# A fused attention and mixture-of-experts kernel: the list of expert tiles made in two parts, the shared expert inside the attention steps

## The reference, cut to what matters

```
x = x + attention(layernorm(x), ctx) + ctx          # per batch: theta, phi, softmax, g, norm over the batch, relu, out
n = layernorm(x)                                    # 2048 tokens of 256
scores = softmax(n @ Wg.T)                          # 16 experts in 4 groups
topi   = top 4 experts within the best 2 groups
y = sum over topi of scores * (silu(n @ W1.T) * (n @ W3.T)) @ W2.T      # 176 hidden columns per expert
z = (silu(n @ Ws1.T) * (n @ Ws3.T)) @ Ws2.T                             # the shared expert, 352 hidden columns
out = x + y + z
```

## Time and profile before

| what | value |
|---|---|
| median of 3 runs | 393.83 us |
| the profiled execution | 395.37 us, of which the profiled span is 393.2 us |
| busy in the span | PE 315.7 us (80%), DVE 254.3, ACT 189.5, POOL 188.1 |
| attention steps and shared expert units | 0 to 223 us |
| first matmul of an expert tile | 222.98 us |
| tiles at an even pace of 1.61 us | 257 to 355 us |
| loading back the ranks, sums, output | 354.8 to 393.2 us |

### The profile page before, as it was taken

The page is one execution under the profiler, slowest core; times in us unless marked ns, Lnnn a source line. Parts: engine busy times, 40 slices in busy tenths (PEclk is TensorE's granted clock), DMA queues, the critical chain, the costliest instruction groups (busy, mean ns, idle before and its releaser), DMA issues.

```text
span 393.2 us, 9572 instructions
## 1 busy us (share of the span) xinstructions
PE 315.7 (80%) x2620; PEld 242.3 (62%) x2621; DVE 254.3 (65%) x923; ACT 189.5 (48%) x473; POOL 188.1 (48%) x223
## 2 busy tenths in 40 slices
PE   0699899967999399954559885499999999999573
PEld 0377577746777287643448653377777777777352
DVE  3456877768775977776877461266665666665584
ACT  0555756652656335742210251366766666665410
POOL 1543332100565235663155665756665666665450
PEclk9999999986989778965589999699999999999969
DMA  8902312220243332352128687688768866678996
GB/s 282 370 14 72 121 65 66 66 64 14 97 130 116 108 92 84 101 203 71 56 92 302 169 181 145 155 146 165 157 143 138 172 149 149 157 172 259 342 323 219
DMA packets 82540, 58.28 MB, mean 148 GB/s; under 512 B 58954, under 2 KB 75981, under 8 KB 82512
## 3 DMA queue, kind: packets, MB, share of 16 engines
q1 hardware_dynamic: 62928, 38.81, 36.6%
q0 software_dynamic: 6912, 17.84, 15.1%
q10 hardware_dynamic: 12672, 1.27, 2.6%
HBM read 24.97 MB, written 24.53 MB: 126 GB/s over the span
## 4 chain that ended last, share of the span: by engine, by line
PE 23%; DVE 8%; SPq 8%; issue 7%; DMA 6%; POOL 5%; ACT 0%; DVEq 0%; ACTq 0%; POOLq 0%
PE banks L815 9%; PE bank L833 8%; POOL slot_rows L1577 5%; SPq L481 4%; PE bank L815 3%; DMA slot_rows<-rows_all,slot_k 3%; SPq L470 3%; DMA w<-ranked 2%; DVE x_all L1515 1%; DMA ranked<-ctx_all 1%; DVE w L1091 1%; SPq L475 0%; PE banks L821 0%; PE bank L821 0%; PE banks L823 0%
## 5 line engine op out<-in xcount | busy, mean ns | idle before, releaser
L1641 POOL DMA_INDIRECT ranked<-ctx_all x80 | 84.0, 1050 | 53.3 <-issue 36.5
L1577 POOL DMA_INDIRECT slot_rows<-rows_all,slot_k x64 | 63.9, 998 | 31.7 <-issue 16.6
L815 PE MATMUL banks<-w,ctx_all 128*128 x324 | 57.3, 313 | 3.8 <-DMA ctx_all<-slot_rows 3.8
L833 PE MATMUL bank<-w,hT 128*128 (+1 forms) x400 | 57.8, 277 | 2.2 <-ACT ctx_all L624 2.2
L755 PE MATMUL banks<-xT_all,w 128*118 128x128 f16 (+1 forms) x576 | 45.8, 252 | 0.0
L755 PEld LDWEIGHTS banks<-xT_all,w 128*118 128x118 f16 x576 | 44.6, 165 | 0.4
L624 ACT ACTIVATE ctx_all<-bank,ctx_all 128x256 f32<-128x256 f32 x80 | 37.7, 472 | 9.8 <-DMA ranked<-ctx_all 4.9
L815 PEld LDWEIGHTS banks<-w,ctx_all 128*128 128x128 f16 x324 | 31.2, 98 | 18.1 <-DMA ctx_all<-slot_rows 5.2
L833 PEld LDWEIGHTS bank<-w,hT 128*128 128x128 f16 (+1 forms) x400 | 36.3, 99 | 5.5 <-issue 2.5
L1382 DVE TENSOR_TENSOR hh<-hid,hh 128x48 f16<-128x48 f32 x80 | 16.7, 208 | 34.5 <-ACT hh L592 34.1
L592 ACT ACTIVATE hh<-hid 128x176 f16<-128x176 f32 x80 | 27.9, 349 | 16.5 <-DVE hid L1378 15.5
(11 more groups left out here) (174 smaller groups left out, 673.7 us busy)
## 6 DMA issues: line engine op xcount, KB each, us to landing
wst<-w_dram SPq DMA_DIRECT2D x18, 608.0 KB, 4.0
w<-ranked SPq DMA_DIRECT2D x16, 512.0 KB, 9.6
x_all<-x_dram SPq DMA_DIRECT2D x4, 512.0 KB, 7.8
ctx_all<-ctx_dram SPq DMA_DIRECT2D x1, 1536.0 KB, 10.7
out_dram<-x_all SPq DMA_DIRECT2D x3, 512.0 KB, 4.1
slot_rows<-pad_rows SPq DMA_DIRECT2D x9, 144.0 KB
ctx_all<-slot_rows ACTq DMA_DIRECT2D x80, 1.0 KB
ranked<-ctx_all POOLq DMA_INDIRECT x80
```

The source lines that it names most:

```text
L815: i = mm(U[j][:, 0:UP1], xt(2 * part + k), up_at(wcol, k, wpart), start=k == 0 and (wpart, part) == (0, 0), stop=k == 1 and wpart == 1)
L833: i = mm(y[:, 0:T], hT[0:rows, j, k * P:(k + 1) * P], down_at(wcol, rows, col), start=start and n == 0, stop=stop and n == len(DOWN) - 1)
L1577: G.indirect_dma_start(scatter_rows, bass.IndirectOffsetOnAxis(ap=slot_k[:, b * TOPK + k:b * TOPK + k + 1], axis=0), rows32[:, b * ROW32:( ...
L1641: G.indirect_dma_start(ranked, bass.IndirectOffsetOnAxis(ap=pair(m)[1], axis=0), y_sb[:, m % YR, :], None, bounds_check=(TOPK + 1) * TOKEN ...
```

## The change

The list of tiles is made twice. The first table has 32 tiles (`FIRST_TILES`), all of them full, from the tokens of the first twelve batches; it is made in the attention steps 18 to 20. The second has the other 48 and is made in expert turns 6 to 12, after the group of batches 12 to 15, whose slots are now computed in turns 3 and 4. Counted on the reference's routing, the first twelve batches fill 40 tiles, and the thresholds of `done_i` (the tiles after which a rank is complete: 60, 64, 68, 72) are the same in both kernels. All 16 shared units are in the steps; unit 15 goes down and is added in turns 0 and 2. Batches 8 to 11 are routed as the loop routes its groups. The pads move from in front of the tiles to SP in front of tiles 16 and 24. POOL sends 48 of its 64 scatters before the tiles, 6 before the first placed tile and 10 between placed tiles 1 to 19. The expert loop of PE has 24 turns in its body instead of 32.

```diff
-FUSED = 10
+FIRST_TILES = 32
-        EARLY = B - 2 * Q
+        EARLY = B - Q
@@ SP
-            issue_pads(sp, 0, NE // 2)
-            sp.wait_ge(S["table_ready"], 1)
-            sp.wait_ge(S["scattered"], 16 * EARLY * TOPK)
-            sp.wait_ge(S["tails_in"], 16 * (NE + 1))
+            sp.wait_ge(S["scattered"], 16 * EARLY * TOPK)
+            sp.wait_ge(S["table_ready"], 1)
...
-            for t in range(2 * MR):
+            for t in range(FIRST_TILES):
+                if t in (2 * MR, 3 * MR):
+                    issue_pads(sp, (t - 2 * MR), (t - MR))
                 if t % 4 == 0:
                     first = load_four(sp, row_i[:, t:t + 4], SLOTS)
-                    sp.wait_ge(places_landed, sp.value_load(places_i[:, t + 3:t + 4], min_val=1, max_val=TOPK))
                 load_tile(t, t % MR, first[t % 4])
-            sp.wait_ge(places_landed, TOPK)
+            sp.wait_ge(S["table_ready"], 2)
+            sp.wait_ge(last_scattered, 16 * (B - EARLY) * TOPK)
+            sp.wait_ge(S["tails_in"], 16 * (NE + 1))
@@ ACT, step
                 tile(s, v, 2, exps)
+                group(s, v, 9, route_exp)
                 tile(s, v, 5, copy_xT)
-                tile(s, v, UP_LAG, shared_tanh, count=FUSED)
+                tile(s, v, UP_LAG, shared_tanh)
                 tile(s, v, 1, theta_phi)
                 tile(s, v, 2, copy_pT)
-                if isinstance(s, int) and s >= B:
-                    tile(s, v, 10, lambda b, u: u == 0 and route_exp(b))
-                else:
-                    group(s, v, 9, route_exp)
@@ DVE, step
                 group(s, v, 10, slots_by_rank)
-                routing(s, v, route_sum)
+                group(s, v, 9, route_recip)
+                group(s, v, 9, route_score)
+                group(s, v, 9, group_max)
+                if isinstance(s, int) and s == B + 3:
+                    full_tiles()
                 tile(s, v, 3, latent_out)
-                routing(s, v, route_recip)
...
@@ DVE, expert turns
+                if r is None and s == 2:
+                    shared_add(B - 1, (B - 1) % 4)
+                if r is None and s == 3:
+                    slots(b0)
+                    count_tokens()
                 estep(s, v, r)
+                if r is None and s == 3:
+                    slots_by_rank(b0)
+                if r is None and s == 4:
+                    slots_sum(b0)
+                    slots_out(b0)
+                if r is None and s == 6:
+                    tiles_up_to(P - 1)
+                if r is None and s == 7:
+                    other_tiles()
+                if r is None and s == 8:
+                    other_rows()
@@ DVE, the first table
+            def full_tiles():
+                V.memset(ones_e[:, :], 1.0)
+                tiles_up_to(0)
+                V.tensor_scalar(taken[:, :], ntc[:, :], float(FIRST_TILES), None, ALU.min)
+                V.tensor_scalar(still[:, :], ntc[:, :], float(FIRST_TILES), -1.0, ALU.min, ALU.mult)
...
+                tile_rows(first_t, 0)
@@ POOL
-                tile(s, v, 11, scatter_two(0), count=EARLY)
+                tile(s, v, 11, scatter_two(0), count=EARLY - 3)
...
+            for b in range(EARLY - 3, EARLY):
+                for k in range(TOPK):
+                    send(b, k, S["scattered"])
+            sends = iter([(b, k) for b in range(EARLY, B) for k in range(TOPK)])
             routed(EARLY)
-            send_place(0, EARLY, B - Q)
...
+            for _ in range(6):
+                send(*next(sends), last_scattered)
...
-            for t in range(MR):
-                place_tile(t, t)
+            for t in range(LONG):
+                place_tile(t, t % MR)
+                if t % 2 == 1 and t < 20:
+                    send(*next(sends), last_scattered)
```

More of the change, by code:

```diff
@@ L743, in router, with shared_up @@
                 i.then_inc(S["l_mm"], 1)
-            def shared_up(b, u, chunks=range(SC)):
-                of = units_at(b) if isinstance(b, int) else UX
+            def shared_up(b, u):
+                if isinstance(b, int) and b == B - 1:
+                    pe.wait_ge(SH["h_ready"], b)
                 if isinstance(b, int) and b == 0:
                     pe.wait_ge(S["wl_ready"], 2)
-                for chunk in chunks:
+                for chunk in range(SC):
                     for half in range(2):
@@ L784, in step @@
                 tile(s, v, 3, mean_all)
-                drain = isinstance(s, int) and s >= B + 2
-                if not drain:
-                    group(s, v, 10, count)
-                if isinstance(s, int) and s == B + 2:
-                    pe.wait_ge(S["thph_ready"], B)
-                    pe.wait_ge(S["p_ready"], B)
-                    shared_up(FUSED, FUSED % 4, (0,))
+                group(s, v, 10, count)
                 tile(s, v, 1, theta)
                 tile(s, v, 5, transpose_rows)
-                tile(s, v, UP_LAG, shared_up, count=FUSED)
+                tile(s, v, UP_LAG, shared_up)
                 tile(s, v, 1, phi)
@@ L895, in estep @@
                     weights.load(s - 4, step_v - 4)
+                if r is not None and step_v == FIRST_TILES - LONG:
+                    pe.wait_ge(S["table_ready"], 2)
                 if has(s, 0) and step_v % 4 == 0:
@@ L1020, in latent_all @@
                 dve.wait_ge(S["st_mm"], b + 1)
-                if u == 3 and not isinstance(b, int):
+                if u == 3 and (not isinstance(b, int) or b == B - 1):
                     dve.wait_ge(S["pre_mm"], b - 3)
@@ L1252, in shared_add @@
                 xs = x_all[:, span(b * T, T)]
-                V.tensor_tensor(xs, sum_at(b) if isinstance(b, int) else YG, xs, ALU.add).then_inc(SH["y_ready"], 1)
+                V.tensor_tensor(xs, YG, xs, ALU.add).then_inc(SH["y_ready"], 1)
             def step(s, v):
-                if isinstance(s, int) and s >= B + 2:
-                    return drain(s)
+                ending = isinstance(s, int) and s >= B + 2
                 late(s, v, 5, low)
@@ L1262, in step @@
                 tile(s, v, 3, latent_stats)
-                tile(s, v, ADD_LAG, shared_add, count=FUSED)
+                tile(s, v, ADD_LAG, shared_add)
                 group(s, v, 10, chosen_diff)
@@ L1287, in step @@
                 tile(s, v, 3, latent_out)
-                routing(s, v, route_recip)
-                tile(s, v, 3, weights_low, count=NU)
-                routing(s, v, route_score)
+                group(s, v, 9, group_compare)
+                if not ending:
+                    tile(s, v, 3, weights_low, count=NU)
                 group(s, v, 10, token_weights)
-                routing(s, v, group_max)
+                group(s, v, 9, group_equal)
                 group(s, v, 10, destinations)
-                routing(s, v, group_compare)
+                group(s, v, 9, group_before)
@@ L1295, in step @@
                 group(s, v, 10, slots_sum)
                 tile(s, v, 4, normalise2)
-                routing(s, v, group_equal)
+                group(s, v, 9, group_rank)
                 group(s, v, 10, slots_out)
                 late(s, v, 2, add_context)
-                routing(s, v, group_before)
-                tile(s, v, UP_LAG, shared_gate, count=FUSED)
-                routing(s, v, group_rank)
+                group(s, v, 9, group_choose)
+                if isinstance(s, int) and s == B + 4:
+                    tile_table(1, 0, FIRST_TILES)
@@ L1303, in step @@
+                tile(s, v, UP_LAG, shared_gate)
+                group(s, v, 9, mask_mult)
                 tile(s, v, 2, recip)
-                routing(s, v, group_choose)
-                tile(s, v, UP_LAG, shared_product, count=FUSED)
-                routing(s, v, mask_mult)
+                group(s, v, 9, mask_add)
+                tile(s, v, UP_LAG, shared_product)
+                group(s, v, 9, top_values)
                 tile(s, v, 3, relu_low)
-                routing(s, v, mask_add)
@@ L1376, in hidden @@
+                group(s, v, 9, top_four)
+                group(s, v, 9, top_replace)
+                if ending:
+                    tile(s, v, 3, weights_low, count=NU)
             def hidden(G, n, j, m):
@@ L1604, in step @@
                     tile(s, v, 2, add_context)
-                tile(s, v, 11, scatter_two(2), count=EARLY)
+                tile(s, v, 11, scatter_two(2), count=EARLY - 3)
             for s in range(B + 4):
```

308 lines of the change are left out of this document (93 added, 215 removed).

## The result

The change takes 383.46 us in the median of 4 runs (380.71 to 389.41), the kernel before 395.21 us (392.82 to 397.25): ratio 0.968, 95% interval [0.958, 0.978]. Measured twice more beside other kernels it gave 0.977 [0.967, 0.987] and 0.964 [0.959, 0.969]. The forecast of 379.7 against 393.83 is 0.964. The trace shown here is that of the third measurement, of the same kernel, 382.45 us with a span of 380.6 us.

The account below looks back on a forecast made before the run. It took DVE's wait for ACT's routing exponential to bound loop routing steps and POOL to bound from 188 us. Terms -9.8, +1.3, +3.7 and -9.3 sum to -14.1 us: 393.8 becomes 379.7 us, range 374 to 390.

Parts of the forecast that it names:

- loop steps, exponential in front: Steps 9 and 13: routing exponential ahead of ACT's copy removes DVE's wait; 4.9 us a group with clock, -9.8 us together.
- last steps: Softmax 15 to the last statistics: a routing group and shared units inserted there make 19.24 us into 22.9, +3.7 us.
- T0 to `slot_k`: From tile 0's first up to the last group's `slot_k`: 7.1 us to the fourth product plus 2.0, 9.1 us.
- behind tile 20: Everything after POOL places tile 20, 115 us of turns and final sums: same instructions in both kernels, no change.
- the stall changes its name: Rival, steps 9 and 13: DVE waits for POOL's `rstd` or PE's rows instead, steps stay 15 us; 389.5 us, chance 0.08.
- The clock that comes back: PE's clock behind the loop's routing steps: recovery worth between nothing and 3.5 us a group, taken as 1.2.
- last steps at half clock: Rival, last steps: PE stays near half clock, shared units cost 5.8 us more in four steps; 385.5 us, chance 0.14.
- POOL's order behind the last `rstd`: From last `rstd` to tile 20: 14 sends before the tiles instead of 32, 10 between them; -9.3 us.
- The landing: Time from the start of the last send before the tiles until it has landed: 3.8 us taken.
- Sends beside DVE: Rival, last `rstd` to tile 20: 50 sends and placings take 0.25 us longer each, 12.5 us; 392.2 us, chance 0.03.
- Units don't overlap (slower): Rival, last steps: each unit lengthens its step by 3.5 us, so last `slot_k` decides; 399.4 us, chance 0.06.
- The covers: Hidden work: DVE's routing before tile 0's product (3 us spare), SP's pads (cost 0), turn 32 behind the sends (1 us spare).

Follow-up runs that it names:

- the exponential alone: Kernel before, with ACT's routing exponential put in front of the copy of transposed rows in loop steps 9 and 13 only; ratios 0.983 and 0.975.
- putting it back: The change with the routing exponential again behind ACT's copy in loop steps 9 and 13; 394.18 us, 0.994.
- the sends first: The change with all 16 sends of the last group ahead of the first placed tile, instead of 6; 390.84 us, 0.986.
- the transpose before down: The change with PE's `transpose_h` in step 18 in front of the router and the shared unit's down; 383.08 us, 0.971.
- all three edits: The change with last group's slots ahead of tile 0, step 18's transpose before down, two sends before the last `rstd`; 0.957, then 382.05 us, 0.942.
- The single edits: The change with one edit each: last group's slots ahead of tile 0 (0.966), step 18's transpose before down (0.971), three sends before the last `rstd` (0.962).
- the three sends earlier: The change with three of the 14 sends behind POOL's last `rstd` put in front of it; 380.68 us, 0.962.
- the three edits with late pads: All three edits, with SP's second eight pads moved from in front of tile 24 to behind tile 31; 384.11 us, 0.957.

## Why the prediction was right

The measured median lies in the range, and the order of the steps held. How well each term fits depends on the execution, so both traces of the change are shown that can be compared, the third measurement's and the second's:

| step | predicted | third | second |
|---|---|---|---|
| loop steps, exponential in front | -9.8 | -9.8 (-8.76 less 1.05) | -6.5 (-5.47 less 1.05) |
| of it: routing steps | -3.7 each | -3.76 and -3.61 | -3.76 and -3.61 |
| step 16's unit | +1.3 | +1.05 | +1.05 |
| last steps | +3.7 | +3.2 | +3.0 |
| last `rstd` to T0 | 25.5 | 25.2 | 25.2 |
| T0 to `slot_k` | 9.1 | 10.4 | 10.4 |
| `slot_k` to tile 0 placed | 7.8 | 8.05 | 8.04 |
| tile 0 to tile 20 placed | 38.4 | 39.03 | 40.12 |
| behind tile 20 | 0 | -0.02 | -0.75 |
| ahead of softmax 7 | 0 | +0.42 | +3.44 |
| sum | -14.1 | -12.6 | -6.2 |

(From `rstd` to T0 is counted from POOL's first instruction, at 182.80 in the third trace.) That the loop steps meet the forecast to a tenth is luck of the execution, as the last column shows. By the medians the change is 11.7, 9.0 and 13.7 us faster than before in its three measurements.

- **The stall was the price, and it went entirely.** DVE's sum waited for nothing, the step became 11.4 to 11.6 us (11.5 taken), and in the change no other wait of DVE took its place. Taking the exponential alone and putting it back show that its place decides. With the exponential alone, though, the step was 12.4, since a third of the wait came back as a wait for POOL's `rstd`. That much of the rival "the stall changes its name" is real; in the change, with the rest of the routing in its new order, the wait is not there.
- **The clock that comes back is the uncertain half of the term.** I gave it 1.2 us a group, with 0 to 3.5 as bounds. (The 3.5 had no sum behind it: the 1.46 of the shared unit lies inside the 11.84 stretch, which alone gives 2.4.) It was 2.5 us for both groups together in the third trace, and 0.8 was lost in the second. Nine traces have the change's loop steps. In six of them softmax 7 to 15 took 86.8 to 87.1 us, with 12.0 to 12.1 and 10.6 us for the two steps behind the second routing step; in three (the change's third, the sends first, the transpose before down) it took 83.0 to 83.8, with 10.1 and 8.96. Before they were 11.84 and 10.56. So mostly the clock did not come back, and where it did, it was by 3.3 us behind one group. My reading that the lowered clock *follows* the stall was only half right: with the stall gone, it still fell in most executions. Why one execution keeps it and another does not stays open.
- **The last steps** cost 3.2, 3.0 and, where the clock fell in them, 5.5 us. The rival "last steps at half clock" is real, but an event of single executions, not a state of this kernel: granted 0.82 against 0.54 before.
- **POOL's order behind the last `rstd`** brought 7.4, not 9.3 (6.4 in the second trace, where tile 20 came another 1.1 later). Of the missing 1.9 us, 1.3 are in `slot_k`. The fourth tile's product ends 10.0 us behind T0, not 7.1, and most of that is PE's clock, a term that I did not have. In both kernels PE does the up of tile 0 and then the last unit's down. In the change PE had stood for 9.25 us and did them at a granted clock of 0.50; before, it had stood for 1.53 us and did them at 1.00. The two take 4.50 us instead of 2.36, so 2.1 of the 2.9 us are there before tile 1 begins. Before, then the change (window, then as in the earlier trace rows):

```profile
222.98:225.34 2.36, 2.36 (x14) 1.80 (x15) 0.00 (x0) 1.60 (x2) 1.75 (x3) 1.00 1.01 180
208.00:212.50 4.50, 4.50 (x13) 2.97 (x14) 0.34 (x1) 0.67 (x2) 0.00 (x0) 0.50 0.48 94
```

```profile
223.88 1.46 PE L765 MATMUL bank<-w,hT 118*128 118x256 f32 x6
209.74 2.76 PE L751 MATMUL bank<-w,hT 118*128 118x256 f32 x6
```

```profile
217.66 0.34 DVE L1288 SCALAR_TENSOR_TENSOR hid<-bank,silu 128x176 f32<-128x176 f32 x1
```

  The 0.8 left of it comes with the prefix count on PE and the slots on DVE, which now stand in front of the third and fourth product; `slot_k` then starts 0.4 behind the fourth. For these together, 1.2, I had added 2.0. Another 0.6 is in the way from tile 0 to tile 20, with placings of 1.014 us in the median of 80, not 0.99, and 0.25 between `slot_k` and tile 0.
- **The zero behind tile 20 is a sum of two differences.** From the placing of tile 20 to that of tile 79 the change takes 97.25 us (97.75 in the second trace) and the kernel before 100.61; from there to the end it takes 17.85 (16.62) and before 14.51. I had the whole at no change because the instructions are the same; it came out so because the two differences cancel. What sets either stays open. The placing of tile 79, before and in the change:

```profile
378.69 1.96 POOL L1641 DMA_INDIRECT ranked<-ctx_all  x1 [0.30 <-issue]
362.75 1.26 POOL L1540 DMA_INDIRECT ranked<-ctx_all  x1 [1.00 <-ACT ctx_all L607]
```

- **The landing was mis-sized, and something else paid it back.** I took the mean of three, 3.8 us, over the 2.3 that I had estimated from the figures of the Trainium skill's page "DMA: Bandwidth & Descriptors", section "Anatomy of one DMA — SWDGE (gpsimd) path". The chain shows 2.46 or 2.47 us for this landing in every trace of a kernel with this order: here the page's estimate was nearer than my rows. The two long ones of my rows had SP's pads (from 207.11 on) and the tiles' transposes in flight beside them; that these made them long was not tried. The 14 sends cost 1.35 each (183.90 to 201.39 for 13), 1.1 us more than 1.26 each, and by luck covered the error of 1.3.
- **Sends beside DVE**: median 0.968 us, the longest of the 64 sends 2.232; the rival with 12.5 us is out. The exclusive lock between GpSimd and VectorE, as the Trainium skill's page "SBUF — State Buffer", section "SBUF: two separate sides", has it, does not show as a price a send here. What makes the few long ones was not tried.
- **Units don't overlap (slower)**: out. `slot_k` came at 218.42, far from the 232.1 at which it would decide.
- **The covers held, and were what they were said to be.** DVE's routing was done at 205.72, tile 0's product came at 210.33 (4.61 us of DVE idle ahead of it). The pads cost nothing in the change, since SP's two blocks of 4.89 and 4.62 us lie in front of tiles that POOL holds back anyway. With POOL's hold shortened, PE stood for 1.8 to 4.8 us behind them (6 was my bound). In the change PE did not stand for rows at turn 32.

The range, 374 to 390, holds all medians of the change (383.46, 388.39, 383.27).

The best version here is all three edits: by the medians 1.2 us below the change run beside it (382.05 and 383.27), by the fastest run of each 10 us (372.05 and 382.12); the ratios are 0.942 [0.935, 0.949] and 0.964 [0.959, 0.969]. The single edits, 0.962 to 0.971, can't be told from the change by their times; only their stretches in the traces speak.

## What to carry to other kernels

Look first for an in-order engine that stands at one small instruction whose producer sits behind an unrelated wait on its own engine: moving that one line gave some 70% of what the whole reordering gave (0.017 of 0.023, 0.025 of 0.036). Its price could be read from the trace to about 1 us a step: 3.77 us of wait, 2.8 us of step saved by that line alone, 3.6 to 3.8 together with the new order of the routing. Price a reordering from the marks at which the engines hand over, and keep the clock's share apart as a term with bounds of its own. When the bound is one queue (POOL), write down which work on the others it hides: here SP's pads were free until POOL was shortened. Then 3.5 us of the 6.5 were left with PE standing for SP twice, and moving half of the pads did not give the rest back.

## What the runs showed of the hardware

The same instructions run at different granted clocks in different executions, and in the change PE does the first up of tile 0 at the lower level behind its long wait: 9.25 us of waiting, then 0.50 for 4.50 us, with 1.94 us for that up (10.52 and 1.94 us in the second trace; 1.53 and 1.07 us in the kernel before). In slices 3 to 5 (28 to 58 us), where no edit touches the work, eight of the twelve traces of the table have a slice at 7 or less; the kernel before, the exponential alone in its second run, the sends first and the three sends earlier have none. Two that dip, of the change's second measurement and of the three edits with late pads:

```profile
PEclk9999669996989878996897798989999999999885
```

```profile
PEclk9999579996989888996987799699999999999666
```

Softmax 7 then comes at 79.51 and 78.76 instead of 76.07. A single trace of such a kernel is good for a wait or a gap, and for a total only within 4 to 7 us (spans of 380.6, 387.0 and 387.6 for the change, 383.2 and 387.0 for the exponential alone). The change and the exponential alone, 1% apart, were told apart with six runs each and not with four.
